# First batch's first-attention tiles: minimum taken with a copy into SBUF, as in the other batches

## The reference, cut to what matters

```python
# layer 1: attention with 16 heads of 16 columns; the softmax runs over axis 2,
# and the sum over m takes the weights alone: each row's own v is scaled
att = einsum('blhd,bmhd->blmh', q, k) * scale     # 2048 x 2048 scores for each batch and head
att = softmax(att, axis=2)
opt = einsum('blmh,blhd->blhd', att, v).reshape(b, l, d)
x = layernorm(x + opt @ w_out.T + b_out)

# layer 2: a router picks 4 of 16 heads of 64 columns for each batch, then ordinary attention
dist = softmax(mean(x @ Wr + br, axis=1)); idx = sort(top_k(dist, 4))
score = softmax(einsum('bhqd,bhkd->bhqk', Qs, Ks) / 8); O = einsum('bhqk,bhkd->bhqd', score, Vs)
x = layernorm(x + O @ Wo + bo)
```

## Time and profile before

| | |
|---|---|
| median of 3 runs | 3718.64 us |
| the profiled execution | 3716.13 us, its span 3714.3 us |
| TensorE busy | 3476.6 us (94%) |
| VectorE busy | 3346.4 us (90%) |
| ScalarE busy | 3081.3 us (83%) |
| GpSimd busy | 1802.5 us (49%) |
| mean granted TensorE clock | 0.957 |
| the first batch's A tiles | from 46.0 us to about 698 us of the span |

### The profile page before, as it was taken

One profiled execution on the slowest core, in us unless ns is written; L12 is line 12 of the kernel. 1 busy time (PEld: TensorE's weight loads), 2 busy tenths in 40 slices (PEclk: granted clock), 3 DMA queues, 4 the chain that ended last, 5 costly groups with the idle time before them and its releaser, 6 DMA issues.

```text
span 3714.3 us, 45759 instructions
## 1 busy us (share of the span) xinstructions
PE 3476.6 (94%) x14222; PEld 1281.0 (34%) x14222; DVE 3346.4 (90%) x4883; ACT 3081.3 (83%) x5097; POOL 1802.5 (49%) x1296
## 2 busy tenths in 40 slices
PE   8999999889999999899999999899999999899998
PEld 4323333433333323433332334343333334343333
DVE  7999999999999999879999999879999999567776
ACT  6999999889999999789999998789999998333333
POOL 6233443403444446444444446455454446657775
PEclk9987888999999999899999999899999999899998
DMA  6122222210010001200000001200010000100000
GB/s 204 53 74 83 80 83 70 85 27 18 18 29 18 29 18 32 84 9 29 18 29 18 29 18 42 74 18 21 18 29 18 29 18 22 46 1 12 12 12 12
DMA packets 117221, 142.87 MB, mean 38 GB/s; under 512 B 33394, under 2 KB 100466, under 8 KB 116978
## 3 DMA queue, kind: packets, MB, share of 16 engines
q1 hardware_dynamic: 116978, 139.95, 12.2%
HBM read 89.55 MB, written 50.33 MB: 38 GB/s over the span
## 4 chain that ended last, share of the span: by engine, by line
PE 43%; ACT 29%; DVE 13%; issue 10%; POOL 3%; SPq 0%; DMA 0%; DVEq 0%; POOLq 0%; ACTq 0%
ACT copies L1146 12%; ACT ps L1146 10%; PE ps L1067 9%; PE ps L1082 9%; PE ps L1102 7%; DVE copies L1340 7%; PE ps L1002 7%; PE ps L975 5%; ACT probs L1261 4%; PE ps L960 3%; DVE smax L1408 1%; PE ps L1085 1%; DVE nmax L1343 1%; POOL facc L911 1%; DVE st L1313 1%
## 5 line engine op out<-in xcount | busy, mean ns | idle before, releaser
L1340 DVE TENSOR_SCALAR_CACHE_REDUCE copies<-ps 128x1024 f32<-128x1024 f32 x1536 | 1795.7, 1218 | 76.8 <-PE ps L1002 67.7
L1146 ACT ACTIVATE copies<-copies,nmax 128x1024 f32<-128x1024 f32 x1536 | 1750.2, 1142 | 105.0 <-DVE copies L1340 94.3
L1002 PE MATMUL ps<-stack 96*128 96x512 bf16 x4550 | 1309.1, 400 | 109.6 <-ACT ps L1146 28.9
L911 POOL TENSOR_TENSOR facc<-facc,probs 128x1024 f32<-128x1024 f32 x443 | 1049.2, 2368 | 574.1 <-ACT probs L1261 507.5
L1002 PEld LDWEIGHTS ps<-stack 96*128 96x128 bf16 x4550 | 345.3, 99 | 1199.9 <-DVE copies L1340 410.4
L1408 DVE TENSOR_REDUCE smax<-ps 128x2 f32<-128x1024 f32 x512 | 621.5, 1221 | 119.9 <-PE ps L1067 119.3
L1067 PE MATMUL ps<-fk,fq 64*128 64x512 f32 x2048 | 566.5, 635 | 51.3 <-ACT probs L1261 33.0
L1343 DVE TENSOR_REDUCE nmax<-ps 128x1 f32<-128x1024 f32 x512 | 586.1, 1216 | 18.6 <-PE ps L1002 17.2
L1146 ACT ACTIVATE ps<-ps,nmax 128x1024 f32<-128x1024 f32 x512 | 561.9, 1161 | 41.5 <-DVE nmax L1343 41.5
L1082 PE MATMUL ps<-fq,fk 64*128 64x512 f32 x2048 | 549.6, 615 | 8.6 <-DVE probs L1438 2.6
L1102 PE MATMUL ps<-probs,vals 128*64 128x512 f32 x2048 | 528.3, 612 | 4.0 <-ACT probs L1261 3.6
(11 more groups left out here) (138 smaller groups left out, 2556.8 us busy)
## 6 DMA issues: line engine op xcount, KB each, us to landing
stack<-qk_levels SPq DMA_DIRECT2D x768, 64.0 KB, 2.2
qk_levels<-fk SPq DMA_DIRECT2D x64, 384.0 KB, 2.5
probs<-in_L_attn_x SPq DMA_DIRECT2D x16, 512.0 KB, 3.9
v_rows<-vals SPq DMA_DIRECT2D x16, 512.0 KB, 2.7
vrows<-v_rows SPq DMA_DIRECT2D x16, 512.0 KB, 3.4
res<-in_L_attn_x SPq DMA_DIRECT2D x16, 512.0 KB, 3.9
x_rows<-y SPq DMA_DIRECT2D x16, 512.0 KB, 2.9
res<-x_rows SPq DMA_DIRECT2D x16, 512.0 KB, 3.9
```

What stands on the lines that cost most here:

```text
L911: pool.tensor_tensor(total, total, probs[:, slot, :], ALU.add).then_inc(facc_ready, 1)
L1002: last = pe.matmul(bank(banks[i]), stack[0:SK, hd % 2, 0, t * P:(t + 1) * P], stack[0:SK, hd % 2, 1, col:col + CH], start=True, stop=True)
L1146: act.activation(src, src, ACT.Exp, bias=nmax[:, b % 2, half, t, hd:hd + 1], scale=-1.0, accum_out=esum[:, b % 2, half, t, hd:hd + 1]).the ...
L1340: dve.tensor_scalar(copies[:, i % COPIES, :, :], two_banks(banks), 1.0, None, ALU.mult, ALU.min, accum_out=lowest_of).then_inc(min_ready, 1)
```

## The change

All A tiles are copied. The planned cost of a copied tile on VectorE goes from 1.23 to 1.17 us, for the tiles of all four batches.

```diff
 def copied(b, j):
-    return b > 0
+    return True
...
             if copied(b, j):
-                unit(dve("A", b, j), 1.23, [pe("A", b, j)] + ([act("A", *through[-COPIES])] if len(through) >= COPIES else []))
+                unit(dve("A", b, j), 1.17, [pe("A", b, j)] + ([act("A", *through[-COPIES])] if len(through) >= COPIES else []))
                 through.append((b, j))
```

## The result

The changed kernel takes 3700.64 us (median of 5 runs, 3696.36 to 3701.32) against 3718.64 us, ratio 0.995 with a 95% interval of 0.9938 to 0.9962. That is 18 us faster; 3708 us was forecast. The profiled execution has a span of 3695.2 us, 19.1 us less than before.

The account below looks back on a forecast made before the run. From 160 to 628 us no engine was full; TensorE waited for ScalarE to free banks, and projections at half clock caused stops. First batch -7.6 and orders -3 gave -10.6 us: 3708 us forecast, range 3690 to 3726.

Parts of the forecast that it names:

- ScalarE's tile +0.042 us, ScalarE the fuller engine: First batch: ScalarE's tile from SBUF takes 0.042 us longer, about 22 us over 512 tiles; ScalarE decides from 160 to 628 us.
- VectorE's copy at 1.14 us a start, the accumulator read hidden: First batch: copied minima start 1.14 us apart, 0.013 us more than plain ones; the 0.08 us accumulator read costs nothing.
- Three buffers shorten the stop at a projection: First batch's projections: three waiting tiles, 3.4 us of work, shorten stops of 2.3 to 2.7 us.
- With tiles waiting, the planner's `queued` is seldom empty, so more tiles are issued twice: First batch: TensorE busier between projections, so four projection matmuls take 1.88 us and not 3.78; clock rises from 0.83 towards 0.95.
- First batch -7.6 us: First batch's sum: 9.5 us saved from 160 to 628 us, less 1.2 before and 0.7 after; the saving reaches the end.
- The new planned cost: Batches 1 to 3: 1.17 for 1.23 changes only the orders; 3 us gained, 39 us the most to be gained.
- a sign of being wrong: First batch gains as forecast, but batches 1 to 3 give it back or add as much again.
- The larger gain by orders: Rival: first stage saves 16.4 us less 1.9, plus a third of later batches' 39 us idle; -28, 3691 us; chance 0.14.
- the slower rival: First batch's projections: half-clock bursts and stops stay, ScalarE's 22 us are added; +20, 3739 us at worst; chance 0.07.
- Worse orders: Rival: new orders lose up to 27 us in the later batches against 7.6 gained, 3738 us; chance 0.05.

Follow-up runs that it names:

- the two other plans with nearly this order: Changed kernel with planned copy cost 1.14: 3681.44 us, ratio 0.9905; copies at 1.23 with ScalarE's first-batch cost 1.19: 3713.88 us, ratio 0.9993.

## Why the prediction was right or wrong

The time was inside the range and on the forecast side; the gain was 18 us where 10.6 were worked out. By its steps:

- *ScalarE's tile +0.042 us, ScalarE the fuller engine.* Right: +0.037, and 97.6% busy where 98.5% was taken.
- *VectorE's copy at 1.14 us a start, the accumulator read hidden.* Right: busy time over count is 1.156 us from 100 to 700 us, 0.011 above the plain minimum.
- *Three buffers shorten the stop at a projection.* The stop did shorten, 2.69 us to 1.21, and ScalarE's waits for minima fell from 31.8 to 9.1 us between 160 and 628 us. That the buffers did it is argued: no run separates them from the new order, and at 1.23 the same buffers went with a loss of 18.1 us.
- *"With tiles waiting, the planner's `queued` is seldom empty, so more tiles are issued twice"* and the clock rises. Wrong. The plan's repeats of the first batch fell from 173 to 14, the clock from 0.83 to 0.78, and bursts of 3.1 to 3.8 us for four matmuls stayed. A copied tile that waits for a buffer has not arrived at VectorE in the plan, so it doesn't count as queued. This happens when ScalarE is the fuller engine in the plan: at 1.23 alone 129 repeats are planned, with ScalarE at 1.19 beside it 13. What the step hoped for is worth having all the same: with the repeats brought back, the last join moved 12.3 us.
- *First batch -7.6 us.* Measured -6.7 at the last join. The size came out although one of its two reasons was wrong: ScalarE came to 97.6% with shorter stops and a lower clock. Part of that may be luck, since the two other plans with nearly this order end 8.0 us earlier and 7.4 us later.
- *The new planned cost*, "I take 3 us gained", with the waits at the changes from batch to batch set aside as waits "which no order removes". This is the mis-sized term: it came to 12.4 us, 1.8 in the batches 1 to 3 and 12.8 in the change from the last batch's tiles to its second attention, less the 2.2 behind it. The prediction had named as a sign of being wrong that batches 1 to 3 would add as much again as the first gains; with the change behind batch 3's tiles counted in, they did. I had looked for the new order's worth in the stages where VectorE is nearly full, and there it stayed small. The path runs through VectorE's scalings in that last change, and an order can move them out of GpSimd's way.
- *The rivals.* The larger gain by orders was the nearest in direction, but its place was wrong too. Of the slower rival (half clock unchanged, stops unchanged) the half clock did stay; the stops were shortened nevertheless. At the cost of 1.23 the kernel was 0.5% slower, but not in this rival's way: ScalarE's waits for minima were 13.0 us there, and VectorE waited 28.9 us for tiles.
- *Worse orders.* That an order can lose 25 us in the first batch (718.3 against 693.4 us) was not among the rivals: the price of the planned cost had been asked for the batches 1 to 3 alone, though the change alters it in the first batch as well, from 1.165 for a plain tile.

## What to carry to other kernels

When a change alters a planner's number, price the orders by the serial changes between stages too, and look in them for instructions whose duration differs several times between calls of the same line: four pieces in 1.38 or 6.33 us is a wait that no wait list shows. Where a rule of the planner decides on extra work that keeps TensorE's clock up, read how the rule counts before saying which way the clock will go. And test an edit and its tuned constant apart: here the edit alone, at the number it came with, lost 21 us of span (3735.3 against 3714.3) where the constant alone gained 14 (3700.2).

## What the runs showed of the hardware

VectorE's scaling of 128 x 256 float32 from SBUF to SBUF takes 0.40 us beside an idle GpSimd, up to 2.57 us beside a busy one, and 0.54 us in the accumulator form in either case; even single VectorE operations on 128 x 4 values grew from 0.16 to 2.27 us. ScalarE's exponential with a sum takes 1.10 us of busy time when it works in PSUM and 1.14 us in SBUF. Ahead of the projections of the first batch, with tiles issued once each, the burst of four matmuls ran at half clock (3.46 us); with tiles issued twice in rows of tiles the mean granted clock of the stretch was 0.98 to 1.00, and eight matmuls took 3.70 us.
